# RMS attention: half turns by row shuffle and row sums by block transposes, both on VectorE, and two banks for attended values

## The reference, cut to what matters

```python
q = _rmsnorm(x @ Wq)            # over all 256 columns
k = _rmsnorm(x @ Wk)
v = x @ Wv
q = (q * qcos + _rotate_half(q) * qsin)      # _rotate_half: [-x2, x1]
k = (k * kcos + _rotate_half(k) * ksin)
q = q * scale                   # 1 / sqrt(16)
logits = jnp.einsum('btkgh,bskh->bkgts', q, k)
probs = jax.nn.softmax(logits, axis=-1)      # not causal
enc = jnp.einsum('bkgts,bskh->btkgh', probs, v)
return enc.reshape(b, t, N * H) @ Wout
```

## Time and profile before

| what | us |
|---|---|
| median of 3 runs | 1579.04 |
| range of the runs | 1576.71 to 1581.8 |
| profiled execution | 1580.17 |
| its span on the core | 1578.4 |
| mean granted clock of TensorE | 0.986 |

### The profile page before, as it was taken

The page is one execution under the profiler, slowest core; times in us unless marked ns, Lnnn a source line. Parts: engine busy times, 40 slices in busy tenths (PEclk is TensorE's granted clock), DMA queues, the critical chain, the costliest instruction groups (busy, mean ns, idle before and its releaser), DMA issues. The chain is left out here.

```text
span 1578.4 us, 29465 instructions
## 1 busy us (share of the span) xinstructions
PE 1459.4 (92%) x10783; PEld 1125.6 (71%) x10810; DVE 978.5 (62%) x2186; ACT 754.7 (48%) x1876; POOL 561.0 (36%) x556
## 2 busy tenths in 40 slices
PE   6999999999899899999999989998998898999897
PEld 4778777787689677777777757985555696633586
DVE  5766667665674766566565657567674754376763
ACT  5565655746235334343433434543454462577352
POOL 2835528363137165435142103532000371100074
PEclk9999999999999999999999999999999999999998
DMA  4122221222363434203031009234000633000434
GB/s 148 60 81 78 89 91 54 71 67 85 135 257 98 164 94 136 72 18 123 0 102 39 1 0 380 73 108 175 2 1 1 222 104 119 1 1 1 185 96 140
DMA packets 54285, 144.89 MB, mean 92 GB/s; under 512 B 9104, under 2 KB 23824, under 8 KB 54032
## 3 DMA queue, kind: packets, MB, share of 16 engines
q1 hardware_dynamic: 36496, 84.99, 15.3%
q0 software_dynamic: 17664, 58.21, 10.9%
HBM read 104.90 MB, written 38.27 MB: 91 GB/s over the span
## 5 line engine op out<-in xcount | busy, mean ns | idle before, releaser
L145 POOL TENSOR_SCALAR ln_var<-ln_moments 128x4 f32<-128x4 f32 x16 | 3.9, 245 | 415.4 <-DVE ln_moments L130 263.2
L412 POOL DMA_INDIRECT expert_rows<-s_y,s_to_row x92 | 91.0, 989 | 58.0 <-ACT s_y L736 37.0
L1370 ACT ACTIVATE s_scratch<-s_bank,s_neg_max 128x128 f32<-128x128 f32 (+3 forms) x128 | 67.2, 528 | 88.2 <-DVE s_neg_max L1460 88.0
L1460 DVE TENSOR_REDUCE s_neg_max<-s_bank 128x1 f32<-128x128 f32 (+3 forms) x128 | 59.4, 486 | 55.1 <-PE s_bank L1260 55.0
L2769 POOL TENSOR_TENSOR s_w_hi<-s_w_raw,zero 128x1024 fp32r<-128x1024 f32 x25 | 55.3, 2214 | 100.4 <-PE s_memory L81 77.1
L1258 PE MATMUL s_bank<-s_k,s_q 128*128 128x128 f32 (+3 forms) x256 | 88.7, 442 | 1.5 <-DVE s_v L1455 0.8
L2454 ACT ACTIVATE s_exps<-s_bank,s_rms 128x512 f32<-128x512 f32 x128 | 76.6, 695 | 20.0 <-PE s_bank L2334 20.0
L953 DVE TENSOR_TENSOR s_h_e<-s_bank,s_silu_e 128x176 f32<-128x176 f32 x92 | 31.4, 341 | 83.6 <-ACT s_silu_e L724 79.7
L79 PE MATMUL s_bank<-xn_t_hi,s_w_hi 128*128 128x512 f32 x192 | 80.3, 418 | 1.3 <-DVE xn_t_lo L212 1.2
L405 POOL DMA_INDIRECT s_xg<-normed_rows,s_from_row x64 | 63.4, 991 | 38.5 <-DVE s_from_row L848 20.2
L1277 PE MATMUL s_bank<-s_probs_t,s_v 128*128 128x512 f32 (+3 forms) x256 | 74.7, 435 | 2.3 <-ACT s_probs_t L1378 2.3
(11 more groups left out here) (426 smaller groups left out, 4915.1 us busy)
## 6 DMA issues: line engine op xcount, KB each, us to landing
s_expert_w_lo<-experts_lo SPq DMA_DIRECT2D x32, 608.0 KB, 13.2
s_e_lo<-in_experts POOLq DMA_DIRECT2D x32, 304.0 KB, 3.1
experts_hi<-s_e_hi POOLq DMA_DIRECT2D x32, 304.0 KB, 2.5
experts_lo<-s_e_lo POOLq DMA_DIRECT2D x32, 304.0 KB, 2.9
s_expert_w_hi<-experts_hi SPq DMA_DIRECT2D x16, 608.0 KB, 12.2
s_w_raw<-in_wa_o SPq DMA_DIRECT2D x16, 512.0 KB, 3.6
s_yg<-expert_rows SPq DMA_DIRECT2D x32, 256.0 KB, 4.7
s_raw<-in_shared SPq DMA_DIRECT2D x16, 384.0 KB, 5.9
```

The costliest lines, as they stand in the source:

```text
L412: pool.indirect_dma_start(out=y_rows[:, :], out_offset=bass.IndirectOffsetOnAxis(ap=to_row[:, i:i + 1].bitcast(U32), axis=0), in_=y[:, i % ...
L1370: act.activation(probs[:, h % 2, r, 0:(r + 1) * P], score_bank(h, r), ACT.Exp, bias=neg_max[:, 4 * h + r:4 * h + r + 1], accum_out=row_sum ...
L1460: dve.tensor_reduce(neg_max[:, 4 * h + r:4 * h + r + 1], score_bank(h, r), AX.X, ALU.max, negate=True).then_inc(max_done, 1)
```

## The change

- The half turn is a row shuffle on DVE (`stream_shuffle`), which permutes the rows inside each block of 32 partitions; the sign is in the table of sines. The matrix `half_turn`, its load and the ten products go. `rotate` waits for ACT's square of that fill in place of the product.
- The row sums: DVE transposes the attended bank in blocks of 32x32 (`transpose`, 128x512), takes the reciprocal of the sums alone (128x16), and transposes them back, spread over 32 rows each. The matrix `sum_sel`, its load, the eight products `finish` and `copy_o` go. `divide` reads the attended bank itself.
- Attended values alternate between two banks; the second is `sum_bank`, used for the small sums before. `attend` waits for `o_done` of unit G-2.
- `project_out(G-1)` stands at step 3 of unit G. DVE's list is `invert`, `divide`, `rotate`, `split_q`. `apply_rms(1)` comes behind the first rotation; the spread is at step 1 of unit 0, and its nine zero products go.
- At the end there are 4 + 4 + 16 zero products in place of 4 + 4 + 23 before the last projection.

```diff
--- before.py
+++ after.py
@@ -2133,7 +2133,7 @@
         sem = ctx.enter_context(Semaphores(nc, name))
         sb = lambda what, shape, dt=F32: ctx.enter_context(nc.sbuf_tensor(f"{name}_{what}", shape, dt))
         banks = [ctx.enter_context(nc.psum_tensor(f"{name}_bank{i}", [P, HALF], F32)) for i in range(8)]
-        acc, s_bank, o_bank, sum_bank = banks[:2], banks[2:6], banks[6], banks[7]
+        acc, s_bank, o_banks, sum_bank = banks[:2], banks[2:6], banks[6:8], banks[7]
         norm = Norm(nc, ctx, sem, f"{name}_ln", res, [b[:] for b in s_bank], measured="first")
         following = Moments(sem, "next_ln", res)
 
@@ -2142,7 +2142,7 @@
         w_raw = sb("w_raw", [P, PER_KV, GQ_COLS])
         w_hi, w_lo = sb("w_hi", [P, PER_KV, GQ_COLS], F32R), sb("w_lo", [P, PER_KV, GQ_COLS], F32R)
         cos, sin = sb("cos", [P, S]), sb("sin", [P, S])
-        half_turn, sum_sel, bv = sb("half_turn", [P, P]), sb("sum_sel", [P, P]), sb("bv", [P, P])
+        bv = sb("bv", [P, P])
         low_rows = sb("low_rows", [P, 1])
         ones = sb("ones", [P, 2])
         square = sb("square", [P, 2, S])
@@ -2150,12 +2150,13 @@
         power, rms = sb("power", [P, 2 * TB]), sb("rms", [P, B, 2, TB])
         qk = sb("qk", [P, FILLS, TOK])
         scaled = sb("scaled", [P, B, 2, S])
-        turned_part = sb("turned_part", [P, S])
+        half_turned, turned_part = sb("half_turned", [P, S]), sb("turned_part", [P, S])
         k_hi, k_lo = sb("k_hi", [P, TOK], F32R), sb("k_lo", [P, TOK], F32R)
         q_hi, q_both = sb("q_hi", [P, S], F32R), sb("q_both", [P, 2, S], F32R)
         v = sb("v", [P, NT, P])
         exps = sb("exps", [P, 2, KV_HEADS, S])
-        o_raw, inverse, o = sb("o_raw", [P, S]), sb("inverse", [P, S]), sb("o", [P, S])
+        by_query, by_query_inverse = sb("by_query", [P, S]), sb("by_query_inverse", [P, S // SLOT])
+        inverse, o = sb("inverse", [P, S]), sb("o", [P, S])
         o_hi, o_lo = sb("o_hi", [P, S], F32R), sb("o_lo", [P, S], F32R)
 
         kv_loaded, w_loaded, loaded = sem("kv_loaded"), sem("w_loaded"), sem("loaded")
@@ -2166,11 +2167,11 @@
             sem("fill_ready"), sem("fill_copied"), sem("fill_squared"), sem("fill_summed"))
         v_ready, v_done, sums_read, rms_step, rms_done = (
             sem("v_ready"), sem("v_done"), sem("sums_read"), sem("rms_step"), sem("rms_done"))
-        rms_spread, rms_applied, half_turned, half_read, cos_part, rotated = (
-            sem("rms_spread"), sem("rms_applied"), sem("half_turned"), sem("half_read"), sem("cos_part"), sem("rotated"))
+        rms_spread, rms_applied, turn_done, sin_part, cos_part, rotated = (
+            sem("rms_spread"), sem("rms_applied"), sem("turn_done"), sem("sin_part"), sem("cos_part"), sem("rotated"))
         k_hi_done, k_lo_done, q_hi_done, q_split = sem("k_hi_done"), sem("k_lo_done"), sem("q_hi_done"), sem("q_split")
-        scores_ready, exp_done, o_ready, o_copied, sum_spread, inverse_done, o_done = (
-            sem("scores_ready"), sem("exp_done"), sem("o_ready"), sem("o_copied"), sem("sum_spread"),
+        scores_ready, exp_done, o_ready, sums_turned, sums_inverted, inverse_done, o_done = (
+            sem("scores_ready"), sem("exp_done"), sem("o_ready"), sem("sums_turned"), sem("sums_inverted"),
             sem("inverse_done"), sem("o_done"))
         o_hi_done, o_lo_done, out_done, acc_read = sem("o_hi_done"), sem("o_lo_done"), sem("out_done"), sem("acc_read")
         pair = lambda hi, lo, *at: (hi[(slice(None), *at)], lo[(slice(None), *at)])
...
@@ -2287,24 +2288,12 @@
                                      res.ident[:], start=j == 0, stop=True, skip_group_check=True)
                 last.then_inc(rms_spread, 1)
 
-            def half(b, f, bank):
-
-                pe.wait_ge(fill_copied, fills.index((b, f)) + 1)
-                pe.wait_ge(half_read, turn_of(b, f))
-                pe.matmul(bank[:], half_turn[:], qk[:, f, batch(b)], start=True, stop=True,
-                          skip_group_check=True).then_inc(half_turned, 1)
-
             pe.wait_ge(ones_made, 1)
             for m in range(FILLS):
                 fill(m)
-                if m == 2:
-                    pe.wait_ge(loaded, 16 * 6)
                 if m:
                     sum_squares(m - 1)
-                if m == 2:
-                    half(0, PER_KV, o_bank)
             sum_squares(FILLS - 1)
-            half(0, 0, o_bank)
             values(0)
             fill(FILLS)
             fill(FILLS + 1)
@@ -2314,8 +2303,6 @@
             for m in range(FILLS + 2, len(fills)):
                 fill(m)
                 sum_squares(m - 1)
-                if m == FILLS + 2:
-                    half(1, PER_KV, o_bank)
             values(1)
             sum_squares(len(fills) - 1)
 
@@ -2341,23 +2328,16 @@
                 b = G // PER_KV
                 pe.wait_ge(exp_done, 4 * (s + 1))
                 if j == 0:
-                    if G:
-                        pe.wait_ge(o_copied, G)
+                    if G >= 2:
+                        pe.wait_ge(o_done, G - 1)
+                    elif G:
+                        pe.wait_ge(rms_applied, 2)
                     else:
-                        pe.wait_ge(half_read, 3)
                         pe.wait_ge(v_done, 2 * B)
                 for g in range(KV_HEADS):
-                    last = pe.matmul(o_bank[slot(g), :], v[:, b * TB + j, slot(g)], exps[:, s % 2, g, :],
+                    last = pe.matmul(o_banks[G % 2][slot(g), :], v[:, b * TB + j, slot(g)], exps[:, s % 2, g, :],
                                      start=j == 0, stop=j == TB - 1, skip_group_check=True)
                 last.then_inc(o_ready, 1)
-
-            def finish(G):
-
-                pe.wait_ge(o_copied, G + 1)
-                if G + 2 < UNITS:
-                    pe.wait_ge(half_read, 3 + G + 2)
-                pe.matmul(sum_bank[:], sum_sel[:], o_raw[:], start=True, stop=True,
-                          skip_group_check=True).then_inc(sum_spread, 1)
 
             def project_out(G):
                 b, c = divmod(G, PER_KV)
...
@@ -2387,26 +2360,16 @@
                     scores(s, 1)
                     if s:
                         attend(s - 1)
-                    if G == 0 and j == 0:
+                    if G == 0 and j == 1:
                         pe.wait_ge(sums_read, 2)
-                        keep_busy(pe, res, sum_bank[:], 9)
                         spread_rms(1, sum_bank)
-                    if G == 0 and j == 1:
-                        pe.wait_ge(rms_applied, 2)
-                        next_half(0)
-                    if G and j == 0 and G + 1 < UNITS:
-                        next_half(G)
-                    if G >= 2 and j == 1:
-                        project_out(G - 2)
-                    if G and j == 2:
-                        finish(G - 1)
+                    if G and j == 3:
+                        project_out(G - 1)
             pe.wait_ge(exp_done, 4 * (TB * UNITS - 1) + 2)
             keep_busy(pe, res, s_bank[0][:], 4)
             attend(TB * UNITS - 1)
             keep_busy(pe, res, s_bank[0][:], 4)
-            project_out(UNITS - 2)
-            finish(UNITS - 1)
-            keep_busy(pe, res, s_bank[0][:], 23)
+            keep_busy(pe, res, s_bank[0][:], 16)
             project_out(UNITS - 1)
             keep_busy(pe, res, s_bank[0][:], 9)
 
@@ -2473,7 +2436,7 @@
             dve.tensor_tensor(w_lo[:, :, wq], w_raw[:, :, wq], f32(w_hi[:, :, wq]), ALU.subtract).then_inc(wq_split, 1)
             norm_low(2)
             norm_low(3)
-            dve.wait_ge(loaded, 16 * 6)
+            dve.wait_ge(loaded, 16 * 4)
 
             def add_ones(b):
                 for h in range(2):
@@ -2493,17 +2456,21 @@
                 dve.tensor_tensor(scaled[:, b, 0, :], bank[:], cos[:], ALU.mult)
                 dve.tensor_tensor(scaled[:, b, 1, :], bank[:], sin[:], ALU.mult).then_inc(rms_applied, 1)
 
-            def rotate(b, f, bank):
+            turn_rows = [SLOT // 2 * (i // HD) + (i + HD // 2) % HD for i in range(SLOT)]
+
+            def rotate(b, f):
                 n = turn_of(b, f)
                 to_cos, to_sin = (cos[:], sin[:]) if f == PER_KV else (scaled[:, b, 0, :], scaled[:, b, 1, :])
                 now = qk[:, f, batch(b)]
                 if f < PER_KV:
                     dve.wait_ge(rms_applied, b + 1)
-                dve.wait_ge(half_turned, n + 1)
+                dve.wait_ge(fill_squared, fills.index((b, f)) + 1)
                 dve.wait_ge(rotated, n)
-                dve.tensor_tensor(turned_part[:], bank[:], to_sin, ALU.mult).then_inc(half_read, 1)
+                dve.stream_shuffle(half_turned[:], now, turn_rows).then_inc(turn_done, 1)
+                dve.wait_ge(turn_done, n + 1)
                 dve.tensor_tensor(now, now, to_cos, ALU.mult).then_inc(cos_part, 1)
-                dve.wait_ge(half_read, n + 1)
```

(55 more changed lines are left out.)

## The result

The changed kernel takes 1569.13 us (median of five runs, 1565.67 to 1572.26), the kernel before 1579.04 us in the same comparison: 9.9 us less. The comparison's ratio is 0.9925 with a 95% interval of 0.9903 to 0.9946, which is 11.8 us; the two medians alone give 0.9937. In a second comparison the ratio was 0.9953 (0.9931 to 0.9974), which is 4 to 11 us. The forecast was 1566.4 us, 12.6 us less: the first interval holds it, the second does not.

A forecast was written before the change was run, and what follows sets the result against it. The prediction took TensorE and ScalarE, alternating over four banks, to bound the attention stage. Savings of 2.6 (projections), 7.05 (loop) and 2.9 us (tail) made 12.6 us, so 1566.4 us; range to hold 8 in 10: 1561 to 1573.5.

The forecast's parts named there:

- What bounds the stage: RMS attention stage: scores and exponentials alternate over four banks; each step ends on TensorE or ScalarE, whichever is last.
- The rule of the two legs: Attention loop: a step takes 2.36 us on ScalarE or 2.59 plus extra product on TensorE; unit 11.49 against 12.02 us.
- the term of 2.6 us: Projections before the loop: three half turns leave TensorE at 0.86 us each, 2.6 us saved.
- The 1.7 us given as uncertain either way: Granted clock of TensorE: a short stretch at 0.50 may go or another come, 1.7 us of work either way.
- Unit 0: First unit of the loop: no projection, but the second batch's spread (0.95 us) in step 1; 10.82 us.
- rival C: TensorE's clock falls to 0.50 in the loop; throughout it 39 us, 1606 us; chance 0.06, in part or throughout.
- Its own sign: Profile after, if the forecast is right: a granted clock of 1.00 from the first exponential on.
- Units 1 to 6: Settled units of the loop: 11.49 us each against 12.02, together 68.94 us.
- Unit 7: Last unit, to its step 3: 7.30 us, with ScalarE's 2.94 us standstill, laid to waiting for `copy_o`, gone through two banks.
- Tail: From unit 7, step 3 to the last projection: zero products end last at 9.60 us against 12.50; 2.9 us saved.
- rivals A and B: VectorE's new operations dearer: A, partly covered, 1572.4 us, chance 0.08; B, VectorE becomes the bound, 1591 us, chance 0.04.
- rival D: After the stage: it is shorter, but the next stage's loads or clock take it back; 1575 to 1579 us; chance 0.05.

The follow-up runs named there:

- the split one: The changed kernel with a unit's output projection cut in two pieces, at steps 2 and 3; ratio to the kernel before 0.9946.
- The two experiments with these nine products: Nine zero products put back into the changed kernel: ratio 0.9940, unit 0 11.0 us; the same nine taken from the kernel before: unit 0 13.4 us.
- the best one: The changed kernel with nine zero products back, projection in two pieces, first sequence's addition to the stream earlier; ratios to before 0.9891 and 0.9887.
- the second profile: The changed kernel run once more with nothing changed, profiled in the second comparison; ratio to the kernel before 0.9953.

## Why the prediction was right, point by point

**What bounds the stage: right.** The rule of the two legs, taken from one unit of before, gave 11.49 us for a unit that measures 11.54, 10.7 for the split one (10.83), and 11.65 for the shuffle alone (11.60). Two products gone from a unit are worth 0.5 us, as the prediction said.

**Projections: right in mechanism, the term of 2.6 us came out at 4.0.** The rest is the clock. The stretch at half clock that the earlier trace rows shows was there in all three profiles of kernels with half turns as products, and in five of the ten without. Where it is there, the projections without half turns take 32.2 to 32.8 us, which is the forecast; where not, 30.7 to 31.0. The 1.7 us given as uncertain either way was the right size. What decides whether it falls there was not found, so that it was missing in both profiles of the changed kernel is luck as far as these runs show.

**Unit 0: the step that failed.** The sum had 10.82 us, measured were 13.72. The prediction moved the spread and priced it, but the nine zero products that go with it have no row in its sum. It had the mechanism as rival C, granted clock 0.50 behind waits, priced it for the whole loop, and said that the new waits are below 0.5 us. At this place the wait is 2.69 us. Its own sign, a granted clock of 1.00 from the first exponential on, did not come for unit 0; behind it the clock was 1.00 from 1374 to 1448 us. The two experiments with these nine products show it both ways.

**Units 1 to 6.** Right, except 0.8 us in unit 5. A moved step was followed on PE and on DVE for `o_lo`, but not for its other wait, `acc_read`. Two steps earlier on PE, that wait met an addition that had not moved on DVE.

**Unit 7: right number, half the reason.** 7.3 us as forecast. But the 2.94 us were taken for a stall by one cause; half was the projection, which the prediction counted as moved anyway, and the stall of 1.4 us came from DVE's order. What the second bank does is another thing: at one bank attending waits 0.39 us in every unit, because the division now reads the bank itself.

**Tail: 3.1 us saved, 2.9 forecast.** The zero products end last, as said; in after:

```profile
1460.62 4.49 PE L87 MATMUL s_bank<-zeros 128*128 128x512 bf16 x20
1464.76 0.47 PE L79 MATMUL s_bank<-s_w_hi,s_o_hi 128*128 128x256 f32 x1
```

**VectorE.** 0.72 us for each new operation; rivals A and B did not occur, and the two kernels with added shuffles show where B begins: 1.9 us of slack a unit. The Trainium skill, VectorE: DVE Perf Modes, section "The perf-mode tier table", has the shuffle at one element a cycle only; an estimate of 0.7 us was worked out from it, and the trace of after agrees with 0.72.

**What is passed on: less than all of it (rival D in a small part).** From the last projection to the end the kernel before took 104.7 us, the changed one 105.7 and 106.8, the best one 108.4 and 107.3. The difference arises before the first gather of the next stage (22.0 us after that stage's first load in before, 25.2 in the best one). In the first profile of the best one the low clock there lasts twice as long as in before; in its second it does not, and 1.8 us are given back nonetheless. That cause stays open. Ahead of the stage the profiles differ by several us between executions of unchanged code: its first product starts at 1325.1 to 1334.2 us.

In sum: of 12.6 us, the profile's stage gave 10.1: projections 1.4 more, unit 0 2.9 less, unit 5 0.8 less, the other units 0.3 less, the tail 0.2 more. In the second profile it gave 11.5. The medians moved by 9.9. That this is so near to 10.1 is in part chance, since the whole time also carries what lies ahead of the stage and behind it; and half of what unit 0 lost was hidden by the stretch that was missing in the projections.

## What to carry to other kernels

Where two engines hand banks to one another, find the two legs of a step and ask on which each step ends: a product that leaves a step already waiting for the other engine is worth nothing, and cutting the remaining extra in two neighbouring pieces was worth more than the two products removed. When a step is moved, write down every wait in it and where its producer stands in its own list. Products of zeros are part of the sum: before one is taken out, measure the gap that it leaves, since 2 us of them kept a loss of 1.6 to 2.8 us away.

## What the runs showed of the hardware

A three-operand VectorE operation took 2.73 us in place of 0.75 while GpSimd ran a subtraction of 128x1024, itself 2.62 us and not 2.36; in after:

```profile
1366.17 2.73 DVE L2490 SCALAR_TENSOR_TENSOR s_q_both<-s_q_hi,s_low_rows,s_qk 128x512 fp32r<-128x512 f32 x1
```

```profile
1365.73 2.62 POOL L2225 TENSOR_TENSOR s_w_lo<-s_w_raw,s_w_hi 128x1024 fp32r<-128x1024 f32 x1
```

It ended 0.55 us after the subtraction here, and 0.54 us after it in the kernel with the zero products put back, so it looks as if it had waited for the subtraction to end. In the kernel before, the subtraction ran beside operations that read a bank, and they kept their 0.69 us. It cost nothing here, since DVE waited for the spread afterwards.

The granted clock of TensorE in this stage: all ten waits of 2.31 to 4.08 us in the thirteen profiles, among them those of 2.66, 2.69 and 4.08 us shown above, have 0.50 inside them or at most 1.7 us behind their end. Shorter waits went either way. In unit 7 one of 1.36 us left the clock at 1.00 in before, and one of 1.35 us had 0.50 behind it in the kernel with the shuffle alone; two of 1.64 and 1.67 us in the kernel with four added shuffles left it at 1.00. With one bank it fell in unit 7, where three waits of 0.39 to 0.42 us stood close together; in the other units of that kernel the same three waits left it at 1.00. So the length of a wait alone does not tell, and what else decides was not found.
